# Roots of a final layer norm: the first four row blocks by Newton steps on VectorE, the other twelve in three groups on GpSimd

## The chip, the cores and the metric

The kernel runs on one core of one Trainium2 chip. The metric is the device time of one execution in microseconds. A measurement of this kernel is a median of several executions; the three of the kernel before lie within 3.65 us of each other.

## What is computed

One decoder layer on 4 x 512 tokens of 512 numbers: block-local attention with some global queries, cross-attention, and a mixture of experts with one shared expert, each added to its input and followed by a layer norm. The change lies in the last of the three norms, behind the experts:

```python
def _layernorm(x, axis=-1, eps=1e-05):
    m = jnp.mean(x, axis=axis, keepdims=True)
    v = jnp.var(x, axis=axis, keepdims=True)
    return (x - m) / jnp.sqrt(v + eps)

# routed: the two best of 8 experts for each token, weighted; shared: one expert for all
x = _layernorm(x + _L0_attn_ref(x, ...), axis=-1)
x = _layernorm(x + _L0_xattn_ref(ctx_512, ctx_512, ..., x, ...), axis=-1)
x = _layernorm(x + _L0_ffn_ref(x, ...), axis=-1)
```

The norm has no scale and no shift of its own. The 2048 tokens are 16 row blocks of 128 (NT = 16).

## The kernel before

The engines work in blocks of the program, one behind the other; the last is `experts`. There 39 tiles (NJ = 39) of up to 128 tokens each, sorted by expert, run through a software pipeline. GpSimd gathers a tile's tokens from DRAM (L1762, into `xg`). TensorE, ScalarE and VectorE turn them, multiply them with the expert's weights (each number as a high and a low part; `we_lo`, L1864, is VectorE's subtraction for that) and ScalarE writes the weighted result to `e_y` (L1813). GpSimd adds it to the rows of `x3_dram` with an indirect DMA (L1768, the scatter), which accumulates in DRAM. Each scatter waits until the one before it has landed (`y_added`).

The final norm follows without a barrier, since the kernel waits with semaphores, each engine in its own program order:

- SyncE loads row block n of `x3` once the scatters that touch it have landed (L1746, `x3_in[n]`), and at the end stores the results in the order of n = 0 to 15 (L1752), each when its producer is done, then waits for all (L1753, L1754).
- VectorE takes each block's statistics (L1912) and aggregates them to mean and variance (L1919, `mv_done`).
- GpSimd, behind its last scatter, takes the inverse root in groups of row blocks (`groups`, L1664): add epsilon (L1785, `ve`), negate the mean (L1786, `minus`), the power -0.5 (L1788, `rstd`) and the product (L1791, `nbias`, `bias_done`).
- ScalarE, behind its last `e_y`, computes rstd * x + nbias for blocks 0 to 10 (L1857), VectorE for blocks 11 to 15 (`DVE_ROWS`, L1922). Both wait for `bias_done` of the block's group.

In the program before, the groups are blocks 0-1, 2-3, 4-7, 8-11 and 12-15. `x3` and the results `o` lie in the space of the experts' weights, so the trace calls both `w_all`; `x_dram` is `x3_dram` there, and `stats`, `mv`, `ve`, `minus`, `rstd`, `nbias` and `half` go without their "3".

Two helpers: `need` (L539) waits for a semaphore if the value is positive; `wait_apart` (L55 to L58) waits and then increments a semaphore of its own.

Of the kernel before, what the change touches and what calls it, by code (L numbers as in the profile page):

```python
# [6 lines left out]
P = 128  # L7
# [3 lines left out]
I32 = mybir.dt.int32  # L11
U32 = mybir.dt.uint32
U8 = mybir.dt.uint8
ALU = mybir.AluOpType
# [40 lines left out]
def wait_apart(eng, sem, value, passed):  # L55

    eng.wait_ge(sem, value)
    eng.sem_inc(passed, 1)  # L58
# [477 lines left out]
def need(eng, sem, value):  # L536

    if not isinstance(value, int) or value > 0:
        eng.wait_ge(sem, value)  # L539
# [483 lines left out]
EPS = 1e-5  # L1023
# [7 lines left out]
NT = T // P  # L1031
# [606 lines left out]
def experts(nc, c, w_gate, w_up, w_down, x2_dram, table_dram, x3_dram, out):  # L1638

    with ExitStack() as ctx:  # L1640
        m = Memory(nc, ctx)
# [12 lines left out]
        y = m.sb("e_y", [P, 2, D])  # L1654
# [3 lines left out]
        mv = m.sb("mv3", [P, NT, 2])  # L1658
        ve = m.sb("ve3", [P, NT])
        rstd = m.sb("rstd3", [P, NT])  # L1660
        minus = m.sb("minus3", [P, NT])
        nbias = m.sb("nbias3", [P, NT])
        half = m.sb("half3", [P, 4])
        groups = [slice(a, z) for a, z in ((0, 2), (2, 4), (4, 8), (8, 12), (12, NT))]  # L1664
        DVE_ROWS = range(NT - 5, NT)

        def group_of(n):
            return next(q for q, group in enumerate(groups) if n < group.stop)
# [5 lines left out]
        x3_in = [m.sem(f"x3_in{n}") for n in range(NT)]  # L1674
        stats_done, mv_done, ve_done, minus_done = m.sem("stats3_done"), m.sem("mv3_done"), m.sem("ve3_done"), m.sem("minus3_done")
        rstd_done, bias_done, half_done = m.sem("rstd3_done"), m.sem("bias3_done"), m.sem("half3_done")
        o_done, o_dve_done, o_out = m.sem("o_done"), m.sem("o_dve_done"), m.sem("o_out")
        x3_rows = x3_dram[0:T, :].rearrange("(n p) d -> p n d", p=P)
        out_rows = out.rearrange("b (t p) d -> p (b t) d", p=P)
# [40 lines left out]
        with nc.Block() as block:  # L1720
# [35 lines left out]
            @block.gpsimd  # L1756
            def _(pool):
                def gather(j):
                    pool.wait_ge(s[f"who{j % WHO}"], 16 * (j // WHO) + 16)
                    need(pool, s["turned"], j - XG + 1)  # L1760
                    pool.sem_inc(c.pool_passed, 1)
                    pool.indirect_dma_start(out=xg[:, j % XG, :], out_offset=None, in_=x2_dram[:],  # L1762
                                            in_offset=bass.IndirectOffsetOnAxis(ap=who[:, j, 0:1], axis=0)).then_inc(s[f"x_in{j % XG}"], 16)

                def scatter(j, p):
                    pool.wait_ge(s["y_out"], j + 1)
                    need(pool, s["y_added"], 16 * j)
                    pool.indirect_dma_start(out=x3_dram[:], out_offset=bass.IndirectOffsetOnAxis(ap=who[:, j, 0:1], axis=0),  # L1768
                                            in_=y[:, p, :], in_offset=None, compute_op=ALU.add).then_inc(s["y_added"], 16)

                pool.memset(g[:], 0.0).then_inc(s["padded"], 1)
                pool.memset(half[:], -0.5).then_inc(half_done, 1)
                for j in range(NJ + XG):
                    if j < NJ:
                        gather(j)
                    if j == 1:
                        pool.wait_ge(s["padded"], 1)
                        pool.wait_ge(half_done, 1)
                        pool.memset(w[FCR:P, :].rearrange("p (e n) -> p e n", n=WCOLS)[:, :, WCOLS - D:WCOLS], 0.0).then_inc(s["zeroed"], 1)  # L1779
                    if j >= XG:  # L1780
                        scatter(j - XG, j % 2)
                pool.wait_ge(half_done, 1)
                for q, group in enumerate(groups):
                    wait_apart(pool, mv_done, group.stop, c.pool_passed)
                    pool.tensor_scalar(ve[:, group], mv[:, group, 1], EPS, None, ALU.add).then_inc(ve_done, 1)  # L1785
                    pool.tensor_scalar(minus[:, group], mv[:, group, 0], -1.0, None, ALU.mult).then_inc(minus_done, 1)  # L1786
                    pool.wait_ge(ve_done, q + 1)
                    pool.tensor_tensor(rstd[:, group], ve[:, group], half[:, 0:group.stop - group.start], ALU.pow).then_inc(rstd_done, 1)  # L1788
                    pool.wait_ge(minus_done, q + 1)
                    pool.wait_ge(rstd_done, q + 1)  # L1790
                    pool.tensor_tensor(nbias[:, group], minus[:, group], rstd[:, group], ALU.mult).then_inc(bias_done, 1)  # L1791

            @block.scalar
            def _(act):
                def w_high(base, kind):
                    act.activation(w_hi[kind][:], raw(base, kind), ACT.Copy).then_inc(s[kinds[kind] + "_hi"], 1)  # L1796

                def x_high(j, p):
                    act.wait_ge(s["turned"], j + 1)
                    act.activation(xT_hi[:, p, :], ps_xT[:, p, :], ACT.Copy).then_inc(s["xT_hi_done"], 1)  # L1800

                def silu(j, p):
                    act.wait_ge(s["g_done"], j + 1)
                    act.activation(act_g[:, p, :], ps_g[:, 0:FH], ACT.Silu).then_inc(s["silu_done"], 1)

                def g_high(j, p):
                    act.wait_ge(s["gT_turned"], j + 1)
                    act.activation(gT_hi[:, p, :], ps_gT[:, 0:FC * P], ACT.Copy).then_inc(s["gT_hi_done"], 1)

                def y_store(j, p):  # L1810
                    act.wait_ge(s["y_done"], j + 1)
                    need(act, s["y_added"], 16 * (j - 1))
                    act.activation(y[:, p, :], ps_y[:, p, :], ACT.Copy,  # L1813
                                   scale=who[:, bass.ds(j, 1), 1].bitcast(F32)).then_inc(s["y_out"], 1)

                def down_high(j, base):
                    need(act, s["y_done"], j)
                    w_high(base, DOWN)

                def gate_high(j, base):  # L1820
                    need(act, s["g_done"], j)
                    w_high(base, GATE)

                def up_high(j, base):
                    need(act, s["u_done"], j)
                    w_high(base, UP)

                def one(j, r):
                    p = r % 2
                    if at(j, 1):  # L1830
                        down_high(j - 1, expert_base(act, j - 1))
                    if not is_last(j):
                        x_high(j + 1, 1 - p)
                        base = expert_base(act, j + 1)
                    silu(j, p)
                    if at(j, 1):
                        g_high(j - 1, 1 - p)
                    if not is_last(j):
                        gate_high(j + 1, base)
                    if at(j, 2):  # L1840
                        y_store(j - 2, p)
                    if not is_last(j):
                        up_high(j + 1, base)

                base = expert_base(act, 0)
                gate_high(0, base)
                up_high(0, base)
                x_high(0, 0)
                act.wait_ge(s["zeroed"], 1)
                tiles(act, one)  # L1850
                down_high(NJ - 1, expert_base(act, NJ - 1))
                g_high(NJ - 1, 0)
                y_store(NJ - 2, 1)
                y_store(NJ - 1, 0)
                for n in range(DVE_ROWS.start):
                    act.wait_ge(bias_done, group_of(n) + 1)
                    act.activation(o[:, n, :], x3[:, n, :], ACT.Identity, bias=nbias[:, n:n + 1],  # L1857
                                   scale=rstd[:, n:n + 1]).then_inc(o_done, 1)

            @block.vector  # L1860
            def _(dve):
# [48 lines left out]
                def row_stats(n):  # L1910
                    dve.wait_ge(x3_in[n], 16)
                    dve.bn_stats(stats[:, n, :], x3[:, n, :]).then_inc(stats_done, 1)  # L1912

                row_stats(0)
                for n in range(NT):
                    if n + 1 < NT:
                        row_stats(n + 1)
                    wait_apart(dve, stats_done, n + 1, c.dve_passed)
                    dve.bn_aggr(mv[:, n, :], stats[:, n, :]).then_inc(mv_done, 1)  # L1919
                for n in DVE_ROWS:  # L1920
                    dve.wait_ge(bias_done, group_of(n) + 1)
                    dve.tensor_scalar(o[:, n, :], x3[:, n, :], rstd[:, n:n + 1], nbias[:, n:n + 1], ALU.mult, ALU.add).then_inc(o_dve_done, 1)  # L1922

            @block.tensor
# [142 lines left out]
```

## Time and profile before

| | us |
|---|---|
| median of 3 runs | 1063.64 |
| the three runs | 1061.74, 1063.64, 1065.39 |
| the profiled execution | 1063.53 |
| its span, first to last instruction | 1061.8 |
| TensorE / VectorE / ScalarE / GpSimd busy | 936.7 / 763.1 / 596.2 / 515.0 |
| mean granted TensorE clock, share of full speed | 0.953 |

All times of the trace are counted from the start of the span. An instruction on a row stands with its start, its duration, engine, line of the kernel, operation, and what it writes and reads. PE is TensorE, PEld its weight loads, DVE VectorE, ACT ScalarE, POOL GpSimd, and SP with a q is SyncE's queue. The arrow in brackets behind an instruction says how long its engine stood idle before it and what ended that. Such releasers are inferred from semaphores, and a wait for several is put down to the one that came last. The change concerns the last 45 us alone; the page shows TensorE idle in the last of its forty slices.

### The profile page before, as it was taken

What the parts mean: (1) busy time and instruction counts of PE and PEld (TensorE: products, weight loads), DVE (VectorE), ACT (ScalarE), POOL (GpSimd) and SP (SyncE); (2) the same over time, 40 slices, a digit from 0 to 9 for tenths busy, and PEclk for the clock granted to TensorE, in tenths of its full rate; (3) what the DMA queues carried; (4) which work ended last, traced back from release to release, by engine and by line L of the source; (5) the groups of instructions that cost most, each with busy time, mean ns of one, the idle gap of its engine ahead of it and who ended that gap; (6) DMA issues with size and microseconds to landing.
All of it is one profiled execution on the core that took longest, in us unless ns stands there. A gap on an engine that the chain in (4) does not pass through costs nothing. (4 is left out here: it accounts for less than half of the span.)

```text
span 1061.8 us, 18013 instructions
## 1 busy us (share of the span) xinstructions
PE 936.7 (88%) x5112; PEld 718.2 (68%) x5112; DVE 763.1 (72%) x1347; ACT 596.2 (56%) x913; POOL 515.0 (49%) x458
## 2 busy tenths in 40 slices
PE   5899998799999999965999999992987999999980
PEld 4677886444544444425888888991876899888870
DVE  3425554777777787648887888854777899999984
ACT  3443211567676767744444444441766888888863
POOL 3450000355555556636565555633243576567734
PEclk9999999799999999986999999997998999999995
DMA  7466500634342425202111111122697444334467
GB/s 259 159 221 217 196 1 2 149 89 105 74 117 61 119 61 143 97 28 82 51 53 61 60 59 59 50 70 73 205 282 236 79 77 72 77 72 78 79 159 228
DMA packets 80883, 115.72 MB, mean 109 GB/s; under 512 B 15680, under 2 KB 37056, under 8 KB 80832
## 3 DMA queue, kind: packets, MB, share of 16 engines
q1 hardware_dynamic: 67760, 93.32, 29.0%
q0 software_dynamic: 9760, 20.49, 10.1%
q10 hardware_dynamic: 3312, 1.32, 0.5%
q8 instruction: 23, 0.38, 0.1%
q14 instruction: 28, 0.23, 0.1%
HBM read 74.77 MB, written 40.31 MB: 108 GB/s over the span
## 5 line engine op out<-in xcount | busy, mean ns | idle before, releaser
L1864 DVE TENSOR_TENSOR we_lo<-w_all,we_hi 128x1408 fp32r<-128x1408 f32 (+1 forms) x117 | 192.3, 1672 | 11.6 <-ACT we_hi L1796 10.9
L691 POOL TENSOR_TENSOR pair_sum<-probs 128x2048 f32<-128x2048 f32 x30 | 137.2, 4575 | 110.6 <-ACT probs L863 110.6
L891 DVE TENSOR_REDUCE maxima<-ps_s 128x8 f32<-128x512 f32 x240 | 148.8, 683 | 54.6 <-PE ps_s L743 54.4
L1796 ACT ACTIVATE we_hi<-w_all 128x1408 fp32r (+1 forms) x117 | 165.8, 1420 | 36.7 <-PE e_ps_y L1937 19.9
L863 ACT ACTIVATE probs<-ps_st 128x512 f32<-128x512 f32 x256 | 135.7, 601 | 67.0 <-PE ps_st L801 65.2
L1768 POOL DMA_INDIRECT x_dram<-e_y,who x39 | 99.3, 2547 | 124.5 <-ACT e_y L1813 77.4
L1534 PE MATMUL ps_gu<-sw_hi,x2T_hi 128*128 128x352 f32 (+1 forms) x256 | 88.1, 344 | 2.1 <-issue 1.7
L1534 PE MATMUL ps_gu<-sw_lo,x2T_hi 128*128 128x352 f32 (+1 forms) x256 | 84.0, 328 | 0.0
L1534 PE MATMUL ps_gu<-sw_hi,x2T_lo 128*128 128x352 f32 (+1 forms) x256 | 83.8, 327 | 0.0
L743 PE MATMUL ps_s<-k_more,q_more 96*128 96x512 f32 x160 | 68.7, 434 | 9.6 <-DVE maxima L891 7.8
L1762 POOL DMA_INDIRECT xg<-x_dram,who x39 | 68.4, 1753 | 14.3 <-issue 11.4
L801 PE MATMUL ps_st<-q_more,k_more 128*128 128x512 f32 x160 | 67.6, 425 | 0.2 <-ACT probs L863 0.2
L332 DVE SCALAR_TENSOR_TENSOR qk_ctx<-ps_proj,bias_qk,qk_ctx 128x512 fp32r<-128x512 f32 x32 | 24.0, 750 | 57.9 <-ACT attn L268 39.8
L761 PE MATMUL ps_o<-probs,vu 128*32 128x512 f32 x512 | 64.9, 601 | 0.0
L262 ACT ACTIVATE qk_ctx<-ps_proj,bias_qk 128x512 fp32r<-128x512 f32 x32 | 22.0, 689 | 66.1 <-PE ps_proj L432 66.1
L1937 PE MATMUL e_ps_g<-we_hi,xgT_hi 128*128 128x352 f32 x156 | 55.6, 356 | 2.8 <-DVE we_lo L1864 2.6
L801 PEld LDWEIGHTS ps_st<-q_more,k_more 128*128 128x128 f32 x160 | 30.1, 188 | 40.8 <-issue 23.9
L1937 PE MATMUL e_ps_u<-we_hi,xgT_hi 128*128 128x352 f32 x156 | 53.9, 346 | 0.0
L1937 PE MATMUL e_ps_g<-we_lo,xgT_hi 128*128 128x352 f32 x156 | 52.3, 335 | 0.0
L1937 PE MATMUL e_ps_g<-we_hi,xgT_lo 128*128 128x352 f32 x156 | 52.3, 335 | 0.0
L1534 PEld LDWEIGHTS ps_gu<-sw_hi,x2T_hi 128*128 128x128 f32 x256 | 49.1, 192 | 4.6 <-issue 3.4
L743 PEld LDWEIGHTS ps_s<-k_more,q_more 96*128 96x128 f32 x160 | 31.0, 195 | 29.9 <-DVE maxima L891 20.3
(268 smaller groups left out, 2486.3 us busy)
## 6 DMA issues: line engine op xcount, KB each, us to landing
qk_dram<-qk_ctx SPq DMA_DIRECT2D x32, 512.0 KB, 2.9
q_more<-qk_dram SPq DMA_DIRECT2D x60, 128.0 KB, 3.0
k_more<-qk_dram SPq DMA_DIRECT2D x60, 128.0 KB, 3.1
w_all<-in_L_ffn_w_gate_dram SPq DMA_DIRECT2D x8, 704.0 KB
w_all<-in_L_ffn_w_up_dram SPq DMA_DIRECT2D x8, 704.0 KB
q_first<-qk_dram SPq DMA_DIRECT2D x36, 128.0 KB, 3.1
k_first<-qk_dram SPq DMA_DIRECT2D x36, 128.0 KB, 3.3
x_tile<-in_x_dram SPq DMA_DIRECT2D x16, 256.0 KB, 2.7
```

Of the source, the lines that this page charges most:

```text
L691: pool.tensor_tensor(pair_sum[:, h], probs[:, 2 * h], probs[:, 2 * h + 1], ALU.add).then_inc(added, 1)
L743: pe.matmul(bank(p, x), q4[p][0:BR, j, t * P:(t + 1) * P], k4[p][0:BR, j, :], start=True, stop=True).then_inc(s_done, 1)
L761: last = pe.matmul(ps_o[HD * j:HD * (j + 1), :], vu[:, kc, HD * j:HD * (j + 1)], probs[:, kc, j, :], start=(kc == 0), stop=(kc == TT - 1))
L801: pe.matmul(st_bank(p, s), k4[p][:, j, kc * P:(kc + 1) * P], q4[p][:, j, :], start=True, stop=True).then_inc(st_done, 1)
L863: act.activation(probs[:, kc, j, :], st_bank(p, s), ACT.Exp, scale=SCALE).then_inc(exp_done, 1)
L891: dve.tensor_reduce(by_tile[:, t, j, 1:9], bank(p, x).rearrange("p (g n) -> p g n", n=S // 8), axis=AX.X, op=ALU.max).then_inc(s_reduced, 1)
L1534: last = pe.matmul(out, stationary[a](q), moving[z](q), start=(q == 0 and k == 0), stop=(q == chunks - 1 and k == 2))
L1762: pool.indirect_dma_start(out=xg[:, j % XG, :], out_offset=None, in_=x2_dram[:], in_offset=bass.IndirectOffsetOnAxis(ap=who[:, j, 0:1], ax ...
L1768: pool.indirect_dma_start(out=x3_dram[:], out_offset=bass.IndirectOffsetOnAxis(ap=who[:, j, 0:1], axis=0), in_=y[:, p, :], in_offset=None, ...
L1796: act.activation(w_hi[kind][:], raw(base, kind), ACT.Copy).then_inc(s[kinds[kind] + "_hi"], 1)
L1864: dve.tensor_tensor(w_lo[kind][:], raw(base, kind), w_hi[kind][:].bitcast(F32), ALU.subtract).then_inc(s[kinds[kind] + "_lo"], 1)
L1937: last = pe.matmul(out, stationary[a](q), moving[z](q), start=(q == 0 and k == 0), stop=(q == chunks - 1 and k == 2))
```

## The change

The groups become blocks 0-3, 4-7, 8-11 and 12-15. The first is no longer GpSimd's: right behind the aggregate of block 3, VectorE takes its roots in `early_root`. It adds epsilon, makes a first guess by shifting the bits of the number right by one and taking them from a constant, improves it with three Newton steps of three instructions each, and writes `nbias`. That is thirteen instructions on 128 x 4 numbers; each of the first twelve increments `early_step`, and VectorE waits for that before the next. The thirteenth increments `early_bias`. GpSimd loops over the other three groups with the same four instructions as before. ScalarE waits for `early_bias` ahead of blocks 0 to 3 and for `bias_done`, counted from the second group, ahead of 4 to 10; VectorE waits for the same ahead of 11 to 15. Two tiles of 128 x 4 and two semaphores are added.

```diff
-        groups = [slice(a, z) for a, z in ((0, 2), (2, 4), (4, 8), (8, 12), (12, NT))]
+        groups = [slice(a, z) for a, z in ((0, 4), (4, 8), (8, 12), (12, NT))]
+        guess = m.sb("guess3", [P, 4], I32)
+        newton = m.sb("newton3", [P, 4])
...
+        early_step, early_bias = m.sem("early_root_step"), m.sem("early_bias_done")
...
-                for q, group in enumerate(groups):
+                for q, group in enumerate(groups[1:]):
                     wait_apart(pool, mv_done, group.stop, c.pool_passed)
...
                 for n in range(DVE_ROWS.start):
-                    act.wait_ge(bias_done, group_of(n) + 1)
+                    if group_of(n) == 0:
+                        act.wait_ge(early_bias, 1)
+                    else:
+                        act.wait_ge(bias_done, group_of(n))
                     act.activation(o[:, n, :], x3[:, n, :], ACT.Identity, bias=nbias[:, n:n + 1],
                                    scale=rstd[:, n:n + 1]).then_inc(o_done, 1)
...
+                def early_root(group):
+
+                    k = 0
+
+                    def link(ins):
+                        nonlocal k
+                        k += 1
+                        ins.then_inc(early_step, 1)
+                        dve.wait_ge(early_step, k)
+
+                    y = rstd[:, group]
+                    dve.wait_ge(mv_done, group.stop)
+                    link(dve.tensor_scalar(ve[:, group], mv[:, group, 1], EPS, None, ALU.add))
+                    link(dve.tensor_scalar(guess[:], ve[:, group].bitcast(I32), 1, None, ALU.logical_shift_right))
+                    link(dve.tensor_scalar(y.bitcast(I32), guess[:], -1.0, float(0x5F3759DF), ALU.mult, ALU.add))
+                    for _ in range(3):
+                        link(dve.tensor_tensor(newton[:], y, y, ALU.mult))
+                        link(dve.scalar_tensor_tensor(newton[:], newton[:], -0.5, ve[:, group], ALU.mult, ALU.mult))
+                        link(dve.scalar_tensor_tensor(y, newton[:], 1.5, y, ALU.add, ALU.mult))
+                    dve.scalar_tensor_tensor(nbias[:, group], mv[:, group, 0], -1.0, y, ALU.mult, ALU.mult).then_inc(early_bias, 1)
+
                 row_stats(0)
                 for n in range(NT):
                     if n + 1 < NT:
                         row_stats(n + 1)
                     wait_apart(dve, stats_done, n + 1, c.dve_passed)
                     dve.bn_aggr(mv[:, n, :], stats[:, n, :]).then_inc(mv_done, 1)
+                    if n + 1 == groups[0].stop:
+                        early_root(groups[0])
                 for n in DVE_ROWS:
-                    dve.wait_ge(bias_done, group_of(n) + 1)
+                    dve.wait_ge(bias_done, group_of(n))
```

## Rows read from the trace of the kernel before

**Rows 1.** The page: busy us by engine; one costly group, busy and mean ns.
```profile
PE 936.7 (88%) x5112; PEld 718.2 (68%) x5112; DVE 763.1 (72%) x1347; ACT 596.2 (56%) x913; POOL 515.0 (49%) x458
...
L1864 DVE TENSOR_TENSOR we_lo<-w_all,we_hi 128x1408 fp32r<-128x1408 f32 (+1 forms) x117 | 192.3, 1672 | 11.6 <-ACT we_hi L1796 10.9
```

**Rows 2.** Chain of waits, 1019 to the end: start us, duration us, what.
```profile
1029.67 6.96 DMA x_dram<-e_y,who
...
1037.38 4.53 DMA x_dram<-e_y,who
...
1042.66 1.55 POOL x_dram L1768
```

**Rows 3.** Timeline of the engines from 1028 to the end.
```profile
1036.60 0.16 DVE L1919 BATCH_NORM_AGGREGATE mv<-stats 128x2 f32<-128x6 f32 x1
...
1036.97 0.69 ACT L1813 ACTIVATE e_y<-e_ps_y,who 128x512 f32<-128x512 f32 x1 [4.95 <-PE e_ps_y L1937]
...
1043.85 0.40 DVE L1919 BATCH_NORM_AGGREGATE mv<-stats 128x2 f32<-128x6 f32 x2
1044.29 0.23 POOL L1785 TENSOR_SCALAR ve<-mv 128x2 f32<-128x2 f32 x1
...
1045.91 3.16 ACT L1857 ACTIVATE w_all<-w_all,nbias,rstd 128x512 f32<-128x512 f32 x4 [8.25 <-POOL nbias L1791]
...
1047.60 0.24 POOL L1785 TENSOR_SCALAR ve<-mv 128x4 f32<-128x4 f32 x1
...
1049.54 5.04 ACT L1857 ACTIVATE w_all<-w_all,nbias,rstd 128x512 f32<-128x512 f32 x7 [0.48 <-POOL nbias L1791]
1049.59 0.24 POOL L1785 TENSOR_SCALAR ve<-mv 128x4 f32<-128x4 f32 x1
...
1053.55 1.92 DVE L1922 TENSOR_SCALAR w_all<-w_all,rstd,nbias 128x512 f32<-128x512 f32 x4 [1.46 <-POOL nbias L1791]
```

**Rows 4.** Stores in SyncE's queue: issue of blocks 10 and 15; landing of all sixteen.
```profile
1054.61 0.33 SPq L1752 DMA_DIRECT2D out_dram<-w_all  x1
...
1057.07 0.64 SPq L1752 DMA_DIRECT2D out_dram<-w_all  x1
...
DMA to landing us min/median/max: 2.0/2.0/3.0
```

**Rows 5.** Windows: stretch, its us, busy by engine, PEclk, DMA share, GB/s.
```profile
1047.00:1048.00 1.00, 0.00 (x0) 0.00 (x0) 0.00 (x0) 0.87 (x2) 0.69 (x4) 0.50 0.40 154
...
1047.00:1059.60 12.60, 0.00 (x0) 0.00 (x0) 2.47 (x5) 6.98 (x10) 5.45 (x14) 0.50 0.89 332
1052.00:1059.00 7.00, 0.00 (x0) 0.00 (x0) 2.00 (x5) 2.58 (x4) 1.37 (x3) 0.50 1.01 378
```

**Rows 6.** Timeline of VectorE, 725 to 730: small chained steps of the planning.
```profile
725.69 1.32 DVE L1006 TENSOR_TENSOR x_tile<-x_tile 128x1 f32<-128x1 f32 x7
...
729.44 0.20 DVE L1015 SCALAR_TENSOR_TENSOR x_tile<-x_tile 128x39 f32<-128x39 f32 x1
729.67 0.17 DVE L1016 CAST first_row<-x_tile 1x39 int32<-1x39 f32 x1
```

**Rows 7.** Windows, two slices of a microsecond, columns as in rows 5.
```profile
1041.00:1042.00 1.00, 0.00 (x0) 0.00 (x0) 1.00 (x5) 0.00 (x0) 0.00 (x0) 0.50 0.42 74
...
1043.00:1044.00 1.00, 0.00 (x0) 0.00 (x0) 1.00 (x4) 0.00 (x0) 1.00 (x1) 0.50 0.00 0
```

**Rows 8.** Line 1768, ns min/median/max; timelines of GpSimd and VectorE, 1007 to 1011.
```profile
L1768 POOL DMA_INDIRECT x_dram<-e_y,who x39: 1552/2892/2963, 764.4 to 1042.7; - x39
...
1007.52 2.80 POOL L1768 DMA_INDIRECT x_dram<-e_y,who  x1 [1.06 <-ACT e_y L1813]
...
1007.24 3.15 DVE L1864 TENSOR_TENSOR we_lo<-w_all,we_hi 128x1408 fp32r<-128x1408 f32 x2
```

**Rows 9.** Timelines of GpSimd and VectorE, 286 to 291.
```profile
285.72 4.56 POOL L691 TENSOR_TENSOR pair_sum<-probs 128x2048 f32<-128x2048 f32 x1 [2.69 <-ACT probs L863]
...
289.20 1.12 DVE L907 TENSOR_TENSOR m_bar<-m_all,bar_u 128x16 f32<-128x16 f32 x1
```

## Prediction

> **What bounds the kernel now.** I read the page's engine totals first, to have the frame [rows 1]: TensorE is busy 936.7 us, 88% of the span of 1061.8 us. That says nothing about this change, because TensorE has no instruction left in the stretch that the change touches. So I went to the chain of waits of the last 43 us [rows 2]. The chain runs through GpSimd's scatters, one after the other, each held by the landing of the one before; the last is issued at 1042.66, and from 1044.29 [rows 3] the chain is the root work of GpSimd (L1785 to L1791, five groups) until VectorE's last rows. Then the timeline of the same stretch, engine by engine [rows 3]. VectorE has the mean and variance of row block 3 at 1036.60 + 0.16 = 1036.76 and of block 15 at 1043.85 + 0.40 = 1044.25. ScalarE is done with its last expert work at 1036.97 + 0.69 = 1037.66 and then does nothing until 1045.91, since it waits for GpSimd's first nbias. GpSimd can't give it earlier: the roots stand behind the scatters in its queue.
>
> After that ScalarE and GpSimd alternate. Blocks 4 to 10 run without a gap from 1049.54, one every (5.04 - 0.81) / 6 = 0.705 us [rows 3], and SyncE issues the store of block 10 at 1054.61, just behind ScalarE's end at 1054.58. Blocks 11 to 15 are issued faster than they are carried [rows 4]. The DMA engines are full from 1052 on at 378 GB/s [rows 5], that is 262,144 B / 378 = 0.694 us for one block; the last store is issued at 1057.07 and lands 3.0 us later, at 1060.07 [rows 4]. From ScalarE's start on block 4 to the last landing it is 1060.07 - 1049.54 = 10.53 us; the rest, 1.73 us to the span's end and 1.73 us around the span, stays. The profiled execution took 1063.53 us, the median of the runs is 1063.64, so the sum below needs no correction beyond 0.1 us.
>
> **Part 1: roots of blocks 0 to 3 move to VectorE.** Thirteen small instructions come in behind the aggregate of block 3; twelve are chained by a wait on their own end. VectorE's nearest rows are the chained planning steps [rows 6]: seven single-column sums in 1.32 us, 0.19 us each, and a scalar-tensor-tensor of 39 columns 729.67 - 729.44 = 0.23 us ahead of the step behind it. With 0.20 for the six plain steps and 0.23 for the seven scalar-tensor-tensors I get 2.8 us; the ends are 13 x 0.19 = 2.5 and 13 x 0.23 = 3.0. The trace shows no logical shift on VectorE and no product that is written as int32 over 128 partitions; the step of L1016, which turns floats into int32 in the same chain, takes 0.17 us like its neighbours [rows 6], and I price the two alike. So nbias of blocks 0 to 3 is there at about 1036.8 + 2.8 = 1039.6. ScalarE waits on it with nothing else to do and takes four blocks, 3 x 0.705 + 0.81 = 2.9 us, to 1042.5. That must be over by 1046.2, when block 4 comes up; it leaves 3.7 us. Break-even of that cover: a root that takes 6.5 us, 0.50 us for each instruction.
>
> What queues behind the root on VectorE are the statistics of blocks 5 to 15: all 2.8 us later. Aggregates of block 7 then come at 1042.2, of block 11 at 1044.8, of block 15 at 1047.1. GpSimd asks for them at 1044.29, 1046.3 and 1048.3 (next part), so each is there in time, the last with 1.2 us to spare. Behind that spare lies another: SyncE doesn't reach block 12 until about 1052.
>
> **Part 2: GpSimd's groups.** Two groups of two blocks go: from 1044.29 to 1047.60, 3.31 us [rows 3]. The groups of four stay, at 1049.59 - 1047.60 = 1.99 us each, and ScalarE can start on one 1049.54 - 1047.60 = 1.94 us after its first instruction. GpSimd's start doesn't move: it hangs on the scatter's landing at 1041.91, not on statistics. In the chain [rows 2] 0.75 us lie between that landing and the next scatter's start at 1042.66, and 0.75 again ahead of the scatter before it. So ScalarE starts block 4 at 1044.29 + 1.94 = 1046.23 in place of 1049.54: **3.31 us earlier**. Blocks 8 to 11 follow at 1048.2, before ScalarE is through with block 7 (1049.1); blocks 12 to 15 at 1050.2, and VectorE writes these four in 1.92 us, to 1052.2. ScalarE ends block 10 at 1051.3, and SyncE issues its store there. The twelve late blocks are then 7 at ScalarE's pace and 5 at that of the DMA engines, as before.
>
> **Part 3: four stores leave early.** They are 1.05 MB, issued from about 1040.5 to 1042.6. Before, the first data flowed about 1.7 us after ScalarE's first start (the slice from 1047 holds 154 of 378 GB/s: it flows from 1047.6 [rows 5]); so here it flows from 1041.3 to 1044.1. At that time the engines carry the tail of one scatter in the slice from 1041 (74 GB/s), and nothing in the slice from 1043 [rows 7]; the last scatter's descriptors are there only at 1044.2. The gap is nearly made for them. I check the end by volume as well: stores hold 332 GB/s x 12.6 us = 4.18 MB from 1047.0 on, all sixteen blocks; the twelve that are left start at 1047.9, are fed at 0.705 us up to block 10 (1052.1), and six more blocks of 0.694 us end at 1056.3, where before it was 1059.6: 3.3 us, the same.
>
> **Part 4: what the two additions cost the scatter.** The next to last scatter's descriptors are made at 1037.38 to 1038.93, right beside the root, and its landing sets GpSimd's start. L1768 takes 1.55 us with no wide VectorE subtraction running at its start, and 2.80 us when it starts 1.3 us before the end of one [rows 8]; the second subtraction, which begins in the middle, costs nothing. So a scatter waits at its start for the VectorE instruction in progress, and for no other. For a root step that is at most 0.2 us. The ends of this term are 0 and 1.3 us (2.89, the median of all 39, less 1.55); I take 0.1, since the root's steps are an eighth as long as a subtraction. The overlap of the first early store with the scatter's tail I put at 0.1, with ends of 0 and 2.4 us (6.96 against 4.53 us for the scatter that met the row loads and the one that hardly did [rows 2]). Two semaphores and four words of tiles cost nothing that any row shows.
>
> **The sum:** 1063.53 - 3.31 + 0.1 + 0.1 = 1060.4 us, 0.3% less than before.
>
> **The rivals.**
>
> *The scatter comes late.* The root's two-input steps hold up descriptors as the wide subtractions do, for 1.3 us instead of 0.1. GpSimd starts 1.3 later: 1063.5 - 3.3 + 1.3 + 0.1 = 1061.6. For: the overlap in time is there. Against: what holds it in [rows 8] is one long instruction, and here each gives way after 0.2 us. If the late scatter then also meets the four stores in full, 2.4 more: 1064.0, no gain left.
>
> *The root is slow, but hidden only in part.* At 0.63 us a step it ends at 1045.0; ScalarE then runs all eleven blocks in a row, 10 x 0.705 + 0.81 = 7.9 us, to 1052.9 instead of 1054.58: 1061.9.
>
> *VectorE's small steps are locked out (the slower side).* Beside a GpSimd instruction that works in SBUF a small VectorE step stands at 1.12 us instead of 0.17: L907 ends when GpSimd's pair sum ends (285.72 + 4.56 = 290.28) [rows 9]. Thirteen steps at 1.12 are 14.6 us: root at 1051.4, ScalarE's blocks 4 to 10 stand behind it, the aggregate of block 15 comes at 1059.0, its group at 1060.9, VectorE's last row block at 1062.9, its landing at 1065, where it was 1060.07: 1068.5. It turns from gain to loss where the root ends later than 1046.7 (1054.58 less 7.9), 0.76 us a step. For: the step is of the kind that was locked. Against: from 1036.8 to 1039.6 GpSimd runs no arithmetic at all, only the one descriptor generation of 1.55 us, and two VectorE subtractions that ran beside such a one took 3.15 us together, 1.6 each [rows 8], against a mean of 1.67 for their line's 117 [rows 1]. Even one full lock-out of 1.55 us is covered by the 3.7 us.
> The Trainium skill has this as a rule (SBUF — State Buffer, section "Who interferes with whom"): a VectorE instruction with two SBUF inputs and a GpSimd instruction that reads SBUF exclude each other, and the second fully waits for the first. By that rule the ten of the thirteen steps with two inputs could be locked, and the time would be that of this rival if GpSimd were computing; the trace agrees for GpSimd's arithmetic (1.12 us), and doesn't for VectorE beside descriptor generation.
>
> **How the numbers follow.** Forecast 0.80, late scatter 0.08, late scatter that meets the stores 0.03, slow root 0.06, lock-out 0.03. A measurement of this kernel can tell about 0.3% from no change, 3.2 us, and that is where the forecast lies: 3.1 of 3.2. The forecast's own range is 1059.9 to 1061.1 by its terms; three runs of before lay between 1061.74 and 1065.39, so a median may be off by 1.2 and the case reaches from 1058.5 to 1062.3. It is halved by the bound: 0.42 of faster, 0.38 of same. The late scatter, its worse form and the slow root are same with 0.15 or so; the lock-out and a little of noise give 0.05 of slower. The range takes in 1061.9 and some spread above it: 1058.4 to 1062.8.
>
> **What would show it.** After the change: ScalarE's four blocks at about 1039.6 to 1042.5, with four stores landed by 1044.7; thirteen VectorE steps within 2.5 to 3.1 us; the scatter on GpSimd still 1.55 us, at most 1.8; GpSimd's first vector step near 1044.3 and its groups at a pitch of 1.99; seven blocks in a row on ScalarE from 1046.2; DMA engines full from 1048 or so to 1056.3. It is wrong if GpSimd waits for a statistic, if the next to last scatter lands after 1042.2, if a gap opens between ScalarE's blocks 7 and 8, or if the stretch before 1036 us moves.

## The result and the profile after

The changed kernel takes 1058.54 us (median of 20 runs, 1054.50 to 1063.89) against 1063.62 us before (20 runs, 1060.91 to 1069.56). The ratio is 0.9950, 95% interval 0.9935 to 0.9965: 5.3 us less, between 3.7 and 6.9 (5.1 by the medians). The forecast had 3.1 us less, took 3.2 us as the least that such a measurement can tell from nothing, and so gave "same" (0.38 and about 0.15 more) over "faster" (0.42). The whole interval lies below 1: the kernel is faster.

The profiled execution looks like no gain at all: 1063.28 us with a span of 1061.6, where before it was 1063.53 with 1061.8. So where did the time go in this one execution? Here is the timeline of GpSimd in the changed kernel, its last two scatters and the first instruction of each root group (start us, duration us, in brackets the idle time ahead):

```profile
1040.15 1.55 POOL L1771 DMA_INDIRECT x_dram<-e_y,who  x1 [6.37 <-DMA x_dram<-e_y,who]
1045.69 1.55 POOL L1771 DMA_INDIRECT x_dram<-e_y,who  x1 [3.99 <-DVE mv L1946]
1047.31 0.25 POOL L1788 TENSOR_SCALAR ve<-mv 128x4 f32<-128x4 f32 x1
...
1049.33 0.23 POOL L1788 TENSOR_SCALAR ve<-mv 128x4 f32<-128x4 f32 x1
...
1051.30 0.23 POOL L1788 TENSOR_SCALAR ve<-mv 128x4 f32<-128x4 f32 x1
```

The bracket at 1045.69 names an aggregate, but the code has this scatter wait only for its `e_y` and for the landing of the scatter before it. The chain of waits has that landing at 1040.15 + 4.79 = 1044.94, 0.75 us ahead of it, as in the kernel before. The last scatter starts 3.0 us later than in [rows 2], and the first root instruction at 1047.31 instead of 1044.29 [rows 3]. Behind it everything is shorter by as much. From the start of the last scatter to the end of the span it is 1061.6 - 1045.69 = 15.91 us; before it was 1061.8 - 1042.66 = 19.14. I call this length the tail. The profile of one execution thus holds two things: a norm that is 3.23 us shorter, and a part ahead of it that was 3.0 us longer. The two executions part ways early in the experts. The next two fences are GpSimd's timeline from 808 to 832, first before, then after:

```profile
819.92 2.40 POOL L1768 DMA_INDIRECT x_dram<-e_y,who  x1 [5.56 <-DMA x_dram<-e_y,who]
...
827.11 1.59 POOL L1768 DMA_INDIRECT x_dram<-e_y,who  x1 [3.51 <-DMA who<-table_dram]
```

```profile
822.05 1.86 POOL L1771 DMA_INDIRECT x_dram<-e_y,who  x1 [7.00 <-DMA x_dram<-e_y,who]
...
830.05 1.59 POOL L1771 DMA_INDIRECT x_dram<-e_y,who  x1 [4.84 <-ACT e_y L1816]
```

The same two scatters are 2.1 and 2.9 us late, long before any changed instruction; from the second of them to the last scatter the distance stays between 2.4 and 3.1 us. An execution of the kernel before can differ from another as much: in the second profile of that kernel, further down, the scatter that started at 834.13 starts at 832.06.

The norm itself went as the steps said. VectorE, ScalarE and SyncE of the changed kernel, from the timeline (SyncE's single stores from narrow windows):

```profile
1039.06 0.17 DVE L1946 BATCH_NORM_AGGREGATE mv<-stats 128x2 f32<-128x6 f32 x1
1039.26 0.17 DVE L1932 TENSOR_SCALAR ve<-mv 128x4 f32<-128x4 f32 x1
1039.46 0.17 DVE L1933 TENSOR_SCALAR guess<-ve 128x4 int32<-128x4 int32 x1
1039.66 0.17 DVE L1934 TENSOR_SCALAR rstd<-guess 128x4 int32<-128x4 int32 x1
1039.87 0.16 DVE L1936 TENSOR_TENSOR newton<-rstd 128x4 f32<-128x4 f32 x1
1040.07 0.16 DVE L1937 SCALAR_TENSOR_TENSOR newton<-newton,ve 128x4 f32<-128x4 f32 x1
...
1041.64 0.16 DVE L1939 SCALAR_TENSOR_TENSOR nbias<-mv,rstd 128x4 f32<-128x4 f32 x1
...
1041.84 2.93 ACT L1863 ACTIVATE w_all<-w_all,nbias,rstd 128x512 f32<-128x512 f32 x4 [0.88 <-DVE nbias L1939]
...
1049.27 5.04 ACT L1863 ACTIVATE w_all<-w_all,nbias,rstd 128x512 f32<-128x512 f32 x7 [4.51 <-POOL nbias L1794]
```

```profile
1042.68 0.34 SPq L1755 DMA_DIRECT2D out_dram<-w_all  x1
...
1050.11 0.33 SPq L1755 DMA_DIRECT2D out_dram<-w_all  x1
...
1054.34 0.33 SPq L1755 DMA_DIRECT2D out_dram<-w_all  x1
...
1056.80 0.64 SPq L1755 DMA_DIRECT2D out_dram<-w_all  x1
```

The thirteen steps stand 0.19 to 0.21 us apart and take 1041.80 - 1039.26 = 2.54 us, whether they are shifts on int32 or Newton steps. ScalarE is done with its first four blocks at 1044.77, 4.5 us before GpSimd has its first group. Seven blocks follow in a row, as in [rows 3], but 3.6 us after the last scatter's start (1049.27 - 1045.69), where it was 6.9 (1049.54 - 1042.66).

### The profile page after: what moved, and what is told of

The parts are those of the page before. It is cut to its first block and busy times, and to the rows that moved or that the text cites. A ratio compares the mean times of both kernels' runs of the same rounds, so it can differ in the third digit from the quotient of the medians.

```text
span 1061.6 us, 18014 instructions
## 1 busy us (share of the span) xinstructions
PE 936.9 (88%) x5112; PEld 717.9 (68%) x5112; DVE 764.6 (72%) x1360; ACT 596.2 (56%) x913; POOL 518.1 (49%) x450
## 5 line engine op out<-in xcount | busy, mean ns | idle before, releaser
L1765 POOL DMA_INDIRECT xg<-x_dram,who x39 | 72.3, 1853 | 14.3 <-issue 11.4
L1959 PE MATMUL e_ps_xT<-ident,xg 128*128 128x128 f32 x156 | 26.8, 298 | 30.5 <-DMA xg<-x_dram,who 30.0
```

## Experiments

Two theories stood against each other. T: the change acts in the tail alone, 3.2 us, and what the twenty runs had beyond that is spread of the part ahead. L: the changed program as such (its code, two more tiles and semaphores) is also faster ahead of the norm, by the other 1.9 us or so. All ratios below are against the kernel before, measured beside it on the same chip.

**The changed kernel again, twice.** No edit.

> The changed kernel once more. The twenty runs gave 5.1 us less than before, with an interval of 3.7 to 6.9; the profiles show 3.2 us less from GpSimd's first root instruction to the end of the span (17.5 to 14.3), and a stretch from 790 to 825 us that was 3 us later in the changed kernel's profile. Theory T (the change acts in the tail alone, the rest is spread of the stretch in which the expert weights arrive): ratio near 0.997, -3.2 us, and the tail in the profile again 14.3 us long whatever the stretch ahead of it does. Rival L (the two tiles and two semaphores, or the code's new place, also make the part ahead of the norm faster): ratio again near 0.995, -5 us.

Measured: 1060.97 us against 1064.59, ratio 0.9966 (0.9952 to 0.9981). The tail is 1056.0 - 1040.12 = 15.88 us.

> The changed kernel a third time, on the chip of the next three. Two sessions gave ratios of 0.9950 (0.9935 to 0.9965) and 0.9966 (0.9952 to 0.9981). Theory T (only the tail, 3.2 us shorter): 0.9970, and the tail of the profile 14.3 us. Rival L (a further gain of about 1.9 us ahead of the norm, from the changed program): 0.9952.

Measured: 1060.12 us against 1063.65, ratio 0.9967 (0.9953 to 0.9982); tail 1058.4 - 1042.54 = 15.86 us. Two times out of three T's figure came out, and the tail is the same in three profiles within 0.05 us. The two profiles, page and GpSimd's timeline, first of the second run, then of the third:

```profile
span 1056.0 us, 18014 instructions
...
1040.12 1.55 POOL L1771 DMA_INDIRECT x_dram<-e_y,who  x1 [4.28 <-DVE mv L1946]
```

```profile
span 1058.4 us, 18014 instructions
...
1042.54 1.55 POOL L1771 DMA_INDIRECT x_dram<-e_y,who  x1 [4.17 <-DVE mv L1946]
1044.16 0.25 POOL L1788 TENSOR_SCALAR ve<-mv 128x4 f32<-128x4 f32 x1
```

The spans of three profiles of one program, 1061.6, 1056.0 and 1058.4, differ by more than the change is worth; their tails don't.

**The kernel before again.** No edit.

> The kernel before, unchanged, against itself: what two equal kernels show. Both theories: ratio 1.000, and its interval says what is not to be told apart. The profile gives a second look at when GpSimd's norm starts: by T anywhere within 3 us of 1044.3, the tail from there to the end of the span 17.5 us.

Measured: ratio 1.0013 (1.0000 to 1.0025), tail 1060.8 - 1041.68 = 19.12 us, 17.49 from the first root instruction. Two equal kernels came out 0.13%, 1.4 us, apart here. Without this run one would read too much into the 1.9 us.

**Tiles and semaphores alone.**

```diff
         half = m.sb("half3", [P, 4])
+        guess = m.sb("guess3", [P, 4], I32)
+        newton = m.sb("newton3", [P, 4])
+        early_step, early_bias = m.sem("early_root_step"), m.sem("early_bias_done")
```

> The kernel before with the change's two tiles and two semaphores declared and not used; the work is that of before. T: 1.000. L: 0.998, about -1.9 us, the part of the gain that the tail doesn't show.

Measured: ratio 0.9998 (0.9985 to 1.0011), tail 19.17 us.

**The root for nothing.** VectorE computes it at its place into spare tiles, GpSimd keeps its five groups; the output is unaffected.

```diff
+                    y = spare_y[:]
+                    link(dve.tensor_scalar(spare_ve[:], mv[:, group, 1], EPS, None, ALU.add))
...
+                    if n + 1 == 4:
+                        early_root(slice(0, 4))
```

> The kernel before with VectorE's root in its place behind block 3's aggregate, its results in spare tiles and used by nobody; GpSimd keeps all five groups. It has the change's code, semaphores and tiles and the 2.6 us of work on VectorE, without the early start. T: ratio 1.000, tail 17.5 us; the aggregate of block 15 comes 2.6 us later and nobody waits for it. L: 0.998. A rival in which the root's delay of the statistics costs something: slower by up to 2.6 us.

Measured: ratio 0.9997 (0.9978 to 1.0015), tail 1060.3 - 1041.15 = 19.15 us. The root ahead of the statistics of blocks 5 to 15 costs nothing in the tail. VectorE's new code without the early start shows no gain, but its interval is wide. A gain of 1.9 us would be a ratio of 0.9982: the tiles and semaphores don't give it, since it lies outside the first interval. For the code it lies at the low end of the second interval, within it, so there L is made unlikely and not ruled out.

**Four groups, all on GpSimd.**

```diff
-        groups = [slice(a, z) for a, z in ((0, 2), (2, 4), (4, 8), (8, 12), (12, NT))]
+        groups = [slice(a, z) for a, z in ((0, 4), (4, 8), (8, 12), (12, NT))]
```

> One part alone: the groups are blocks 0-3, 4-7, 8-11, 12-15, and all four stay on GpSimd. T by the rows of before: first group's nbias at 1046.2, ScalarE then runs eleven blocks in a row to 1054.1 in place of 1054.6, the stores flow without a gap: -0.5 us, 0.9995. By the rival that the larger groups are what helps, and not the early start: -3 us. By L (a part of the gain comes from a changed program as such): anything like -2 us.

Measured: ratio 0.9990 (0.9979 to 1.0002), tail 1062.7 - 1044.01 = 18.69 us, 0.45 less than before. ScalarE's timeline shows the one row of eleven:

```profile
1047.60 7.86 ACT L1857 ACTIVATE w_all<-w_all,nbias,rstd 128x512 f32<-128x512 f32 x11 [9.42 <-POOL nbias L1791]
```

Closing ScalarE's gaps alone is worth 0.45 us in the tail. The other 2.8 us come from the first four blocks being early. The ratio can't tell the 0.45 us from nothing.

**The early stores held back.** What carries the gain, ScalarE's early work or the early stores?

```diff
-                        sp.wait_ge(o_done, n + 1)
+                        sp.wait_ge(o_done, max(n + 1, groups[0].stop + 1))
```

> The changed kernel, but SyncE issues the stores of blocks 0 to 3 only when block 4 is done; ScalarE still computes them early. If the gain is carried by the DMA engines (four stores fewer in the last stretch): the sixteen stores start to flow where the twelve did, 1048.1 on the scale of the profile of before, and need 11.1 us to 1059.2, so the tail is 17.1 us and the ratio 0.9996. If the gain is carried by ScalarE's early work: tail 14.3 us, ratio 0.997.

Measured: ratio 0.9997 (0.9981 to 1.0013), tail 1059.0 - 1040.52 = 18.48 us. ScalarE still has its four blocks early, and nearly all of the gain is gone: 0.66 us of 3.23 are left. From its windows (columns as in rows 5), the stretch in which the stores flow:

```profile
1046.00:1056.00 10.00, 0.00 (x0) 0.00 (x0) 2.47 (x5) 3.15 (x5) 1.75 (x5) 0.50 1.02 382
```

The DMA engines are full for ten microseconds while ScalarE has only 3.15 us of work left in them. The end is set by bytes: four stores moved out of this stretch are 4 x 0.69 = 2.8 us, and the two tails, 18.48 and 15.88, differ by 2.6.

**A longer root.** How far does the cover reach? More Newton rounds change nothing in the result but its time on VectorE (nine rounds; fifteen and six likewise).

```diff
-                    for _ in range(3):
+                    for _ in range(9):
```

> The changed kernel with nine Newton rounds in place of three: 31 instructions, at the 0.197 us a step of the changed kernel's profile 6.1 us instead of 2.6. On the scale of before the root ends at 1042.9 and ScalarE's block 3 at 1045.8, just ahead of GpSimd's nbias for block 4 at 1046.2; the aggregate of block 15 comes at 1050.4, the last group at 1052.4, VectorE's last block at 1054.3, about when SyncE gets to it. Theory: cover nearly used up and nothing lost, ratio 0.997 (-3.1 us), tail 14.3 to 14.6 us. Rival (VectorE's time is on the path already): +3.5 us against the change, ratio 1.000.

Measured: ratio 0.9998 (0.9978 to 1.0019), tail 1061.4 - 1043.76 = 17.64 us. The root takes 1043.66 - 1037.58 = 6.08 us as reckoned, but the tail is 1.76 longer than the change's, not 0 to 0.3. The expectation was wrong, and GpSimd's row says why. Its timeline, and VectorE's aggregate of block 7:

```profile
1043.76 1.55 POOL L1771 DMA_INDIRECT x_dram<-e_y,who  x1 [3.69 <-DMA x_dram<-e_y,who]
1046.51 0.25 POOL L1788 TENSOR_SCALAR ve<-mv 128x4 f32<-128x4 f32 x1 [1.19 <-issue]
```

```profile
1046.16 0.16 DVE L1946 BATCH_NORM_AGGREGATE mv<-stats 128x2 f32<-128x6 f32 x1
```

GpSimd stands idle for 1.19 us behind its last scatter, and goes on 0.19 us after the aggregate of block 7 has ended. The row names "issue" as the releaser and not VectorE, but its code waits there for that aggregate. It waits for VectorE twice more, at the groups of blocks 8 to 11 and 12 to 15: VectorE needs 4 x 0.66 = 2.6 us for four blocks' statistics, GpSimd 1.99 for a group, so once it has caught up, each next group comes later still.

```profile
1049.15 0.23 POOL L1788 TENSOR_SCALAR ve<-mv 128x4 f32<-128x4 f32 x1 [0.71 <-DVE mv L1946]
...
1051.37 0.34 POOL L1788 TENSOR_SCALAR ve<-mv 128x4 f32<-128x4 f32 x1 [0.33 <-DVE mv L1946]
```

GpSimd's last `nbias` starts 1053.17 - 1043.76 = 9.41 us behind the last scatter, where the change has 1053.04 - 1045.69 = 7.35: 2.06 later. That GpSimd's end counts, line 1723 shows, where the engines meet at the end of the block of the program. Its rows, first of the changed kernel, then with nine rounds (ns three times, then the start in us):

```profile
L1723 POOLq DRAIN  x1: 6695/6695/6695, 1053.0 to 1053.0; - x1
...
L1723 SPq DRAIN  x1: 7/7/7, 1060.1 to 1060.1; - x1
...
L1723 SPq EVENT_SEMAPHORE  x1: 17/17/17, 1060.2 to 1060.2; - x1
```

```profile
L1723 POOLq DRAIN  x1: 6695/6695/6695, 1053.1 to 1053.1; - x1
...
L1723 SPq DRAIN  x1: 7/7/7, 1059.2 to 1059.2; - x1
...
L1723 SPq EVENT_SEMAPHORE  x1: 17/17/17, 1060.0 to 1060.0; - x1
```

GpSimd's queue has a drain that begins with its last instruction and takes 6.69 to 6.70 us in all fourteen profiles; what it does isn't shown. In the changed kernel it is over at 1059.7, 0.4 us before SyncE, which waits for the last store, comes to the same line at 1060.1. With nine rounds it is over at 1059.8, and SyncE is there at 1059.2 and passes only at 1060.0. So the end of the program waits for two things, the last store and GpSimd's drain, and they lie close together. The 2.06 us of delay less this spare are 1.7 us, the longer tail.

> Fifteen Newton rounds: 49 instructions, 9.65 us, where the prediction put the point at which gain turns to loss (a root of 9.9 us). On the scale of before the root ends at 1046.5, ScalarE runs eleven blocks to 1054.4, the aggregate of block 15 comes at 1053.9, its group at 1055.9, VectorE's blocks 12 to 15 at 1056.4 to 1057.8, and the last four stores end at 1060.3 in place of 1059.6. Tail 17.3 to 18.3 us, ratio 1.0006 (0.9998 to 1.0008), no gain left. Rival (the cover is larger than that): ratio under 0.998.

Measured: ratio 1.0025 (1.0006 to 1.0044), slower than before, tail 1063.0 - 1040.86 = 22.14 us. That is 3.0 us more than before's, where 0.2 less to 0.8 more was expected, for the same reason: the last `nbias` starts 13.92 us behind the last scatter. The longest waits of this kernel from 1040 to 1060 (us in total, times, longest):

```profile
ACT w_all L1863 <- DVE nbias L1939: 8.4, 1, 8.4
POOL ve L1788 <- issue: 5.7, 1, 5.7
```

ScalarE waits 8.4 us for the root and is still done with its four blocks at 1048.23, 1.8 us before block 4 comes up; GpSimd waits 5.7 us for block 7.

> The changed kernel with six Newton rounds: 22 instructions, 4.4 us. With nine rounds GpSimd stood 1.2 us at its first group, for the aggregate of block 7, which queues behind the root on VectorE. So the cover ends where that aggregate comes as late as GpSimd asks for it: 1044.29 on the scale of before, against 1039.4 plus the root, a root of 4.9 us and not of 6.5. By this corrected rule 4.4 us still cost nothing: no wait of GpSimd at its first group, tail 14.3 us, ratio 0.997. If every microsecond of the root counts from three rounds on (nine rounds cost 1.7 us in the tail for 3.5 us of root): tail 15.1 us, ratio 0.998.

Measured: ratio 0.9958 (0.9941 to 0.9975), tail 1060.3 - 1043.61 = 16.69 us. GpSimd's first group:

```profile
1043.61 1.55 POOL L1771 DMA_INDIRECT x_dram<-e_y,who  x1 [4.24 <-DVE mv L1946]
1045.42 0.25 POOL L1788 TENSOR_SCALAR ve<-mv 128x4 f32<-128x4 f32 x1 [0.27 <-issue]
```

Here the root takes 1042.57 - 1037.93 = 4.64 us and GpSimd loses 0.2 us: its root instruction starts 1.81 us behind the scatter's start, where 1.62 is the rule (1047.31 - 1045.69). By the rule of that expectation this was all it could lose; but GpSimd waits again at the next two groups, 0.72 and 0.34 us, and its last `nbias` starts 8.47 us behind the scatter, 1.12 later than in the change. So the cover ends near a root of 4.64 - 1.12 = 3.5 us for GpSimd's last group and, with the spare at the end, near 3.9 us for the tail, in this execution. With six, nine and fifteen rounds the tail less the time to the last `nbias` is 8.22, 8.23 and 8.22 us (16.69 - 8.47, 17.64 - 9.41, 22.14 - 13.92): the whole length behind it is GpSimd's. In the three profiles of the change it is 8.53 to 8.56, and the stores end last. The ratio, 0.9958, is even lower than the change's; with an interval of 0.17% to either side, these ratios can't see the 0.8 us that the tails show.

**Roots inside the last gap.** GpSimd waits some 4 us between its last two scatters, for a landing. This version has no root on VectorE and puts two of GpSimd's four groups there.

```diff
-        groups = [slice(a, z) for a, z in ((0, 2), (2, 4), (4, 8), (8, 12), (12, NT))]
+        groups = [slice(a, z) for a, z in ((0, 4), (4, 8), (8, 12), (12, NT))]
...
+                    if j == NJ + XG - 1:
+                        roots(0)
+                        roots(1)
                     if j >= XG:
                         scatter(j - XG, j % 2)
...
+                roots(2)
+                roots(3)
```

> No VectorE root: GpSimd takes the groups 0-3 and 4-7 between its last two scatters, where it waits 3.7 us for a landing, and 8-11 and 12-15 behind the last scatter. Nbias of blocks 0-3 at 1040.9 and of 4-7 at 1042.9 on the scale of before, the last scatter starts 0.2 to 0.4 late, ScalarE runs eleven blocks in a row to 1048.8, and the stores become a plain stream: 1042.6 + 16 x 0.69 us + 0.7 to 2.3 us for the last scatter's packets = 1054.4 to 1056.0 where before it was 1059.6. Expected ratio 0.9958, -4.5 us (-3.6 to -5.2). If the stores then hold up the last scatter's landing or the other way round by more than their bytes: no better than the change, 0.997.

Measured: 1058.13 us against 1063.65, ratio 0.9959 (0.9943 to 0.9975), as forecast.

> The groups 0-3 and 4-7 between GpSimd's last two scatters once more, on another occasion. First time 0.9959 (0.9943 to 0.9975). Expected again 0.9958, and 20.2 us from the start of the next to last scatter to the end of the span, where the changed kernel has 21.5 and the kernel before 24.5. If the first result was luck and it is no better than the change: 0.997 and 21.5 us.

Measured: ratio 0.9962 (0.9945 to 0.9979). From the start of the next to last scatter to the end of the span it is 1055.9 - 1035.69 = 20.21 us, and 20.22 the second time; the change has 21.45, 21.72 and 21.58, the kernel before 24.42 and 24.69. GpSimd in the first of the two profiles, timeline:

```profile
1035.69 1.55 POOL L1768 DMA_INDIRECT x_dram<-e_y,who  x1 [5.34 <-DVE mv L1925]
1037.31 0.25 POOL L1774 TENSOR_SCALAR ve<-mv 128x4 f32<-128x4 f32 x1
...
1041.02 0.20 POOL L1780 TENSOR_TENSOR nbias<-minus,rstd 128x4 f32<-128x4 f32 x1
1041.74 1.68 POOL L1768 DMA_INDIRECT x_dram<-e_y,who  x1 [0.53 <-DVE mv L1925]
1043.49 0.23 POOL L1774 TENSOR_SCALAR ve<-mv 128x4 f32<-128x4 f32 x1
```

By the profiles it beats the change by another 1.2 to 1.5 us; by the ratios (0.9959 and 0.9962 against 0.9950, 0.9966 and 0.9967) that isn't settled. The end lies 8.43 and 8.45 us behind GpSimd's last `nbias`, so only some 0.2 us are left before GpSimd's drain sets it. It has a fault that the change doesn't have: GpSimd waits for the statistics of blocks 0 to 7 ahead of its last scatter. With this routing none of these blocks needs that scatter. With another, in which the last tile holds a token of blocks 0 to 7, it would wait for ever. That was not tried.

## Why the prediction came out as it did

**The mechanism and the tail: right.** The sum had 3.31 us from two groups off GpSimd's queue, and 3.1 with two small costs. The tail shrank by 3.23, 3.26 and 3.28 us against 19.14. ScalarE's block 4 starts 1.96 us after GpSimd's first root instruction (forecast 1.94), its seven blocks take 5.04, the DMA engines carry 376 GB/s behind it (forecast 378), and ScalarE's start on block 4 to the end of the span is 12.33 us against 12.26 before.

**The two small costs: not seen, and the tail couldn't show them.** I had added 0.1 us for descriptors that wait for a root step and 0.1 for stores that meet the scatter. The scatter beside the root takes 1.55 us in all three profiles, as in [rows 2]. From it to the last one it is 5.54, 5.84 and 5.72 us with early stores, and 5.28, 5.57, 5.54, 5.69 and 6.21 in the five kernels without (before twice, tiles alone, root for nothing, four groups). These lengths spread by 0.9 us with no early store, so 0.2 us may hide in them; the tail begins behind them. The late scatter, the rival with 1.3 us, has nothing for it. The locked-out steps neither: the two-input steps beside descriptors are at 0.16 us. Single steps with one input are longer beside them, 0.44 us for L1933 in the second profile, 0.23 for L1934 in the third, 0.51 with six rounds and 0.33 with fifteen, where they take 0.17 otherwise. Why it takes these and not the others isn't shown.

**The call between "same" and "faster": wrong, and this is the step that failed.** The prediction put at 3.2 us, 0.3%, what a measurement of this kernel can tell from no change, and set its 3.1 us against that. No row was given for the 0.3%. The measured intervals reach 0.15% to either side, 1.6 us, half of it: the two repeats gave only 3.6 and 3.5 us less, and their intervals end at 0.9981 and 0.9982, clear of 1. By that width a gain of 3.1 us would have come out as "faster" as well. The 0.2 us of costs, rounded in against bounds that began at 0, moved the forecast from just above the bound to just below it; with the bound where it belongs they would have made no difference.

**The size: 5.3 us for 3.1.** The first twenty runs gave 5.3 us (3.7 to 6.9), two repeats 3.6 and 3.5; the mean ratio of the three is 0.9961, 4.1 us. The tail explains 3.2 to 3.3. The controls for the tiles and semaphores and for VectorE's code give 0.9998 and 0.9997, and equal kernels gave 1.0013. So the surplus is most likely spread, argued and not shown, of the kind that the profiles have between 764 and 834 us. That 1058.54 still lies within the stated range, 0.1 us from its lower end, is owed to what the range had for such spread and not to the sum. One of the prediction's own signs came up by it: the stretch before 1036 us moved, by 3 us, in the profile that showed no gain. Whether some 0.8 us beyond the tail are real stays open: the intervals are as wide as that.

**Part 1's cover: wrong, hidden by a margin that was thinner than it looked.** The text gave the root's cover as 6.5 us, the time until ScalarE must be free for block 4. It had the spares of the statistics behind the root as well, 2.1 us for block 7, 1.5 for block 11 and 1.2 for block 15, but didn't draw the break-even from them: behind the last it saw another spare, SyncE's, which doesn't reach block 12 until 1052. The path that it left out is GpSimd's own: a late block 15 delays GpSimd's last group and with it the drain, which ends at 1060.0 in the kernel before, only 0.3 us before SyncE comes to the same line:

```profile
L1720 POOLq DRAIN  x1: 6695/6695/6695, 1053.3 to 1053.3; - x1
...
L1720 SPq DRAIN  x1: 7/7/7, 1060.3 to 1060.3; - x1
```

By the prediction's rows the cover is then 2.8 + 1.2 = 4.0 us for that group and about 4.3 for the tail, 0.33 us a step. The longer roots bear it out: 4.6 us cost 0.8 us of tail, 6.1 cost 1.8, 9.8 cost 6.3. The change itself had little left in one execution: in the second profile the aggregate of block 15 ends at 1045.01 and GpSimd's last group starts at 1045.72, with some 0.2 us needed between the two. The slow-root and lock-out rivals were priced with the same error; at 0.76 us a step the kernel would have lost, not broken even, as fifteen rounds show (9.8 us, ratio 1.0025).

**The root's price: 2.54 us for 2.8.** The scalar-tensor-tensor on 128 x 4 numbers is not dearer than a plain step; the 0.23 of [rows 6] belong to 39 columns. The shift and the int32 product cost the same 0.17.

**What the early stores do: as said in Part 3**, and the held-back stores show that this is where the gain comes from: 2.6 of 3.2 us go away with them while ScalarE has its four blocks as early as in the change.

## What to carry to other kernels

Where the last stretch of a kernel is a stream of stores at full rate, time is gained by moving bytes out of it, into a gap ahead, not by making the engine that feeds it faster; and the gap may lie in the queue of the engine that already does the work, as in the version with roots between the last two scatters. Work put into an engine's queue must be held against everything behind it that somebody waits for, down to the end of each engine's queue, and each spare written down, since the smallest one decides and not the most visible: here it was that of the last block's statistics, seen and passed over. And before a forecast is called too small to be measured, the width of the intervals should be taken from runs. And where runs of one program differ by more than the change is worth, count from an event shortly ahead of the change to the end: that length repeated here within 0.05 us, while spans differed by 5.6.

## What was not expected of the hardware

Stores alone ran at 375 to 382 GB/s in the kernel before, in the changed one and with the stores held back. In the version with roots in the gap they ran faster, in both profiles. Windows of the first, columns as in rows 5:

```profile
1047.00:1053.00 6.00, 0.00 (x0) 0.00 (x0) 1.91 (x4) 0.65 (x1) 0.52 (x2) 0.50 1.04 402
```

402 GB/s is 0.65 us for a block instead of 0.69. The issues stand 0.4 to 0.9 us apart there and the stores land 3.2 us after their issue in the median, where it was 2.0 before. That more of them are under way isn't enough to explain it: with the stores held back they land after 3.0 us in the median and run at 382. What makes the difference was not tested.

The drain of 6.7 us at GpSimd's end stands in no part of the prediction either. It hides behind the last stores as long as GpSimd's last `nbias` starts more than 8.2 us before the end of the span.
